# An edge product held in PSUM through its mish, in the first aggregation of a GNN kernel

## The chip, the cores and the metric

The kernel runs on one core of a Trainium2 chip. The metric is the device time of one execution in microseconds (us); the median of three runs of the kernel before is 4279.02 us.

## The reference, cut to what matters

The program is a graph network layer, a mixture of experts, a second graph layer and a second mixture, each added to the node features. The change touches the first stage of aggregation, in which two things are computed side by side: the weighted sum of neighbours of the first graph layer, and, for two thirds of the edges, the edge term `y` that only the second graph layer needs later.

```python
# first graph layer: aggregation of transformed nodes over the edges
msgs = support[edge_src] * edge_weight[:, None]
agg = segment_sum(msgs, edge_dst)
# second graph layer: the edge term
mish = lambda x: x * tanh(softplus(x))
y = mish(edge_features @ W_edge.T + b_edge)
```

With z the product plus its bias, the kernel writes tanh(softplus(z)) as 1 - 2/((1+e^z)^2 + 1). It stores (q - 1) * z, which is minus mish(z), where q = 2/((1+e^z)^2 + 1) is made by ScalarE from min(z, 20).

## The kernel before, in words

`stage_conv` is the stage. Its 106250 edges, sorted by target, are cut into groups of 512 (`CG` = 4 columns of 128). Six groups (`SLOTS`) make one round; there are 35 rounds (`IT`). For every group POOL gathers 4 times 128 rows of `support_table` into one of six buffers `gath` (line 509, 832 gathers), VectorE builds a matrix of edge weights at their targets (`one_hots`, lines 542 to 545), TensorE multiplies both into a PSUM tile `ps` (`segment`, line 655), and VectorE adds that tile to the running sums (`add`, line 537).

Between the groups stand four edge products per round (`MISH` = 4, numbered r = 0 to 3): TensorE multiplies a 512-edge block of edge features by `W_edge` into `ps_z[r % 2]` (`product`, line 664, 16 instructions in the profile). There are two such PSUM tiles; with three `ps` tiles and one for transposes they fill PSUM. VectorE then runs `mish_begin`: it adds the bias (line 523) from `ps_z` into the SBUF tile `neg[r]`, signals `z_free[r % 2]`, and clamps (line 525) from `neg[r]` into `q[r]`. ScalarE makes the factor in `q[r]` by four activations (lines 940 to 943). VectorE's `mish_end` multiplies (line 529) into `neg[r]`, which the queue of SP stores to memory (`store`).

The order is written out by hand, the same on each engine. In turn r of a round TensorE runs the groups `BEFORE[r]` (two groups when r is 0 or 2, one when r is 1 or 3) and then `product(r)`, which waits for `z_free[r % 2]`. VectorE, in its turn r, adds those groups, builds one-hots if r is odd, copies out 180 finished rows if r is 3 (`rows_of`, line 552), and then runs `mish_begin` of the product before, r-1, and `mish_end` of the one before that, r-2. At the start of a round VectorE also loads six addresses into registers (`places_of`, line 410). The first two rounds' products and round 0's groups are written out apart in `first()`, with n counting 0 to 7; there TensorE runs `product(n)` ahead of group n.

Of the kernel before, what the change touches and what calls it, by code (L numbers as in the profile page):

```python
# [10 lines left out]
ALU = mybir.AluOpType  # L11
# [3 lines left out]
P = 128  # L15
D = 256
# [10 lines left out]
CG = 4  # L27
# [9 lines left out]
MISH = len(KEPT)  # L37
# [14 lines left out]
ZMAX = 20.0  # L52
# [41 lines left out]
def take(eng, semaphore, n=1):  # L94

    eng.wait_ge(semaphore, n)
    eng.sem_inc(semaphore, -n)  # L97


def link(eng, ins, semaphore):  # L100

    ins.then_inc(semaphore, 1)
    take(eng, semaphore)
# [303 lines left out]
def places_of(nc, window, i, count, whole=False):  # L407

    at = window[0:1, bass.ds(i if whole else i * SLOTS, count)]
    return nc.values_load_multi_w_load_instructions(at, engines=[mybir.EngineType.DVE], min_val=0, max_val=NP)[1]  # L410


def stage_conv(nc, c, table):
# [4 lines left out]
    with ExitStack() as ctx:  # L418
# [9 lines left out]
        bias = sb("bias", [P, D])  # L428
        ln2 = sb("ln2", [P, 1])
        edge = [sb(f"edge{r}", [P, KD, CG * P]) for r in range(MISH)]  # L430
        q = [sb(f"q{r}", [P, CG, D]) for r in range(MISH)]
        neg = [sb(f"neg{r}", [P, CG, D]) for r in range(MISH)]
        ps = [pb(f"ps{n}", [P, W]) for n in range(3)]
        ps_z = [pb(f"pz{r}", [P, CG, D]) for r in range(2)]
# [12 lines left out]
        own, act_own, neg_own = sem("own"), sem("act_own"), sem("neg_own")  # L447
        w_in, act_free = sem("w_in"), sem("act_free")
        per_r = lambda n: [sem(f"{n}{r}") for r in range(MISH)]
        edge_in, edge_free, z_done, z_free = per_r("edge_in"), per_r("edge_free"), per_r("z_done"), [sem(f"z_free{n}") for n in range(2)]  # L450
        z_ready, q_ready, neg_ready, neg_out = per_r("z_ready"), per_r("q_ready"), per_r("neg_ready"), per_r("neg_out")
        block = ctx.enter_context(nc.Block(no_gpsimd_drain=True))

        def load_passes(eng):
            return eng.value_load(c.passes[0:1, 0:1], min_val=1, max_val=TW // W + 1)
# [59 lines left out]
        @block.vector  # L515
        def _(dve):
            def mish_begin(r):
                take(dve, z_done[r])
                dve.sem_inc(edge_free[r], 1)

                take(dve, neg_out[r], 16)

                link(dve, nc.vector.tensor_tensor(neg[r][:], ps_z[r % 2][:], bias[:].unsqueeze(1).to_broadcast([P, CG, D]), ALU.add), neg_own)
                dve.sem_inc(z_free[r % 2], 1)
                nc.vector.tensor_scalar(q[r][:], neg[r][:], ZMAX, None, ALU.min).then_inc(z_ready[r], 1)

            def mish_end(r):
                take(dve, q_ready[r])
                link(dve, nc.vector.scalar_tensor_tensor(neg[r][:], q[r][:], -1.0, neg[r][:], ALU.add, ALU.mult), neg_own)
                dve.sem_inc(neg_ready[r], 1)  # L530

            def add(places, s):
                take(dve, ps_ready[s % 3])
                dve.sem_inc(slot_free, 1)
                here = sums[:, bass.ds(places[s], W)]

                link(dve, nc.vector.tensor_tensor(here, here, ps[s % 3][:], ALU.add), own)
                dve.sem_inc(ps_free[s % 3], 1)

            def one_hots(i, half):  # L540
                part_of = lambda a: a[:, bass.ds(i * (SLOTS * CG) + half * HALF_COLS, HALF_COLS)]
                nc.vector.tensor_copy(at_hot[half][:, 0, :], part_of(rel))
                link(dve, nc.vector.tensor_copy(at_hot[half][:, 1, :], part_of(c.weight)), own)
                for j in range(HALF_COLS):
                    last = nc.vector.scalar_tensor_tensor(hot[half][:, j, :], c.iota[:], at_hot[half][:, 0, j:j + 1],
                                                          at_hot[half][:, 1, j:j + 1].to_broadcast([P, W]), ALU.is_equal, ALU.mult)
                last.then_inc(hot_ready[half], 1)

            def rows_of():
                take(dve, turned_ready)  # L550
                take(dve, rows_out, 16)
                link(dve, nc.vector.tensor_copy(rows[:], ps_t[:]), own)
                dve.sem_inc(rows_ready, 1)

            def step(i, behind):
                if behind:
                    dve.sem_inc(due, 1)
                places = places_of(nc, window, i, SLOTS)
                for r in range(MISH):
                    for s in BEFORE[r]:  # L560
                        add(places, s)
                    if behind and r == 3:
                        rows_of()
                    if r % 2:

                        one_hots(i + 1, r // 2)
                    mish_begin((r - 1) % MISH)
                    mish_end((r - 2) % MISH)

            def first():  # L570
                places = places_of(nc, window, 0, SLOTS)
                for n in range(2 * MISH):
                    if n < SLOTS:
                        add(places, n)
                    if n in (2, 5):

                        one_hots(1, n // 3)
                    if n >= 1:
                        mish_begin((n - 1) % MISH)
                    if n >= 2:  # L580
                        mish_end((n - 2) % MISH)

            for n in range(3):
                dve.sem_inc(ps_free[n], 1)
            for n in range(2):
                dve.sem_inc(z_free[n], 1)
            for r in range(MISH):
                dve.sem_inc(neg_out[r], 16)
            dve.sem_inc(rows_out, 16)
            nc.vector.memset(ln2[:], LN2)  # L590
            nc.vector.tensor_copy(rel[:], c.dstrel[:])
            link(dve, nc.vector.tensor_copy(window[:], c.base[:]), own)
            dve.sem_inc(act_free, 1)
            dve.wait_ge(w_in, 32)
            link(dve, nc.vector.memset(sums[:], 0.0), own)
            with dve.Fori(0, load_passes(dve)) as k:
                for half in range(2):
                    one_hots(0, half)
                first()
                for i in range(1, BEHIND):  # L600
                    step(i, False)
                with dve.Fori(BEHIND, IT - 1) as i:
                    step(i, True)
                places = places_of(nc, window, IT - 1, TAIL)
                add(places, 0)
                mish_begin(MISH - 1)
                add(places, 1)
                mish_end(MISH - 2)
                add(places, 2)
                add(places, 3)  # L610
                for m in range(IT - 1 - BEHIND, IT):
                    dve.sem_inc(due, 1)
                    if m == IT - BEHIND:
                        mish_end(MISH - 1)
                    rows_of()

                nc.vector.tensor_scalar(rel[:], rel[:], -float(W), None, ALU.add)
                link(dve, nc.vector.tensor_scalar(window[:], window[:], float(W), float(NP), ALU.add, ALU.min), own)
# [1656 lines left out]
```

## Time and profile before

| | |
|---|---|
| median of 3 runs | 4279.02 us (4276.55 to 4279.75) |
| profiled execution, span | 4272.1 us |
| its own time beside the span | not listed apart; the median is 6.9 us over the span |
| share of the span busy: PE, PEld, DVE, ACT, POOL | 82%, 72%, 54%, 45%, 66% |
| mean granted TensorE clock | 0.848 of 2.4 GHz |
| the stage of the change | first gather at 104.3 us, last at 1257.0 us; its last sums at 1264 us |

Engines: PE is TensorE's matmuls, PEld its weight loads, DVE is VectorE, ACT is ScalarE, POOL is GpSimd, SP the queue of transfers. The shares are averages over stages with different limits; for this change only the stretch from 104 to 1275 us matters, and what counts there is which wait ends last. The granted clock has two levels, 1.0 (2.4 GHz) and 0.5 (1.2 GHz); a mean between them says how much of a stretch was spent on each.

### The profile page before, as it was taken

The page shows a single profiled execution, that of the slowest core. Times are in us where ns is not written, and L with a number is a line of the kernel's source. Part 1 is how long each engine was busy: PE and PEld are TensorE (multiplying, and loading weights), DVE is VectorE, ACT ScalarE, POOL GpSimd, SP SyncE. Part 2 cuts the span into 40 slices and gives each one's busy share as a digit, 9 for nine tenths or more (in the row PEclk, how much of TensorE's full clock was granted, in tenths as well). Part 3 has the DMA queues.
Part 4 walks back from the last instruction along what each step waited for, and adds up shares of the span by engine and source line. Part 5 has one row for each costly group of instructions (what it writes and reads, how often), then busy time and mean ns, then how long its engine had stood idle before and what let it go on. Part 6 is the DMA issues. An engine that isn't in the chain of part 4 may idle for free. (4 is left out here: it accounts for less than half of the span.)

```text
span 4272.1 us, 68475 instructions
## 1 busy us (share of the span) xinstructions
PE 3514.0 (82%) x17723; PEld 3093.3 (72%) x17723; DVE 2295.0 (54%) x6976; ACT 1939.7 (45%) x3024; POOL 2823.4 (66%) x2732
## 2 busy tenths in 40 slices
PE   4777777777756899999999968888888888649999
PEld 4666666666645788888888867777777777538887
DVE  6566556556554445545445436666666666632222
ACT  4455555555541333333333445555555555423333
POOL 3677777777767777766676227777777777353444
PEclk7788788888776999999999987777777787559999
DMA  6455555555543222222222126666666666534443
GB/s 177 154 187 188 179 174 183 178 180 178 178 140 107 69 68 66 69 66 64 68 67 64 36 96 208 212 206 212 209 209 208 212 211 191 172 137 92 98 98 60
DMA packets 287817, 605.53 MB, mean 142 GB/s; under 512 B 61999, under 2 KB 163342, under 8 KB 287499
## 3 DMA queue, kind: packets, MB, share of 16 engines
q1 hardware_dynamic: 166267, 344.34, 25.0%
q0 software_dynamic: 114784, 245.67, 21.0%
q10 hardware_dynamic: 6576, 13.36, 0.9%
q8 instruction: 74, 1.21, 0.1%
q14 instruction: 116, 0.95, 0.1%
HBM read 460.33 MB, written 144.67 MB: 142 GB/s over the span
## 5 line engine op out<-in xcount | busy, mean ns | idle before, releaser
L1669 POOL DMA_INDIRECT y_node<-node_table,src_sb x832 | 847.6, 1019 | 379.2 <-issue 378.9
L509 POOL DMA_INDIRECT conv_gath<-support_table,src_sb x832 | 878.4, 1056 | 284.3 <-issue 259.9
L1110 POOL DMA_INDIRECT x_gath<-hidden_table,src_sb x832 | 792.9, 953 | 353.6 <-issue 259.9
L664 PE MATMUL conv_pz<-conv_we,conv_edge 128*128 128x256 f32 x2240 | 643.1, 451 | 76.9 <-PEq L97 76.7
L1682 PE MATMUL y_pa<-y_hot,y_node 128*128 128x64 f32 x3328 | 523.6, 326 | 181.7 <-PEq L97 181.1
L1682 PEld LDWEIGHTS y_pa<-y_hot,y_node 128*128 128x128 f32 x3328 | 506.8, 240 | 214.7 <-issue 212.0
L664 PEld LDWEIGHTS conv_pz<-conv_we,conv_edge 128*128 128x128 f32 x2240 | 510.2, 234 | 170.2 <-issue 81.4
L655 PE MATMUL conv_ps<-conv_hot,conv_gath 128*128 128x64 f32 x1664 | 255.6, 305 | 213.5 <-DMA conv_gath<-support_table,src_sb 210.9
L655 PEld LDWEIGHTS conv_ps<-conv_hot,conv_gath 128*128 128x128 f32 x1664 | 242.5, 219 | 245.9 <-DMA conv_gath<-support_table,src_sb 238.5
L1734 ACT ACTIVATE y_node<-y_node 128x1024 f32<-128x1024 f32 x208 | 219.4, 1056 | 340.6 <-ACTq L97 340.1
L1692 PE MATMUL y_pz<-y_we,y_edge 128*128 128x256 f32 x1104 | 361.0, 499 | 13.0 <-PEq L97 13.0
L940 ACT ACTIVATE conv_q<-conv_q 128x1024 f32<-128x1024 f32 x140 | 148.0, 1057 | 488.3 <-ACTq L97 488.3
L746 POOL DMA_INDIRECT out<-e_outs,e_node x112 | 175.0, 1562 | 281.5 <-POOLq L97 264.4
L1692 PEld LDWEIGHTS y_pz<-y_we,y_edge 128*128 128x128 f32 x1104 | 284.1, 264 | 69.2 <-issue 13.4
L1193 PE MATMUL x_ph<-x_xt,x_w 128*128 128x256 f32 (+1 forms) x1296 | 294.1, 371 | 0.5 <-PEq L97 0.3
L1199 PE MATMUL x_pm<-x_hid,x_w 128*128 128x256 f32 (+1 forms) x1296 | 289.7, 368 | 2.0 <-PEq L97 1.9
L1206 PE MATMUL x_py<-x_w,x_mid 128*128 128x256 f32 x1176 | 282.6, 381 | 1.6 <-PEq L97 1.6
L1321 ACT ACTIVATE x_hid<-x_ph,x_b 128x256 f32<-128x256 f32 (+1 forms) x324 | 129.0, 449 | 337.3 <-ACTq L97 337.0
L1127 PEld LDWEIGHTS x_ps<-x_hot,x_gath 128*128 128x128 f32 x1664 | 220.6, 201 | 74.4 <-DMA x_gath<-hidden_table,src_sb 46.3
L1804 DVE TENSOR_TENSOR y_node<-y_node,y_neg 128x256 f32<-128x256 f32 x556 | 199.7, 420 | 131.6 <-DMA y_node<-node_table,src_sb 131.6
L1127 PE MATMUL x_ps<-x_hot,x_gath 128*128 128x64 f32 x1664 | 217.9, 281 | 61.4 <-DMA x_gath<-hidden_table,src_sb 41.5
L1199 PEld LDWEIGHTS x_pm<-x_hid,x_w 128*128 128x128 f32 x1296 | 231.5, 196 | 28.7 <-issue 2.9
(256 smaller groups left out, 5844.8 us busy)
## 6 DMA issues: line engine op xcount, KB each, us to landing
conv_edge<-in_edge_t SPq DMA_DIRECT2D x140, 512.0 KB
edge_mish_table<-conv_neg SPq DMA_DIRECT2D x140, 512.0 KB
y_neg<-edge_mish_table SPq DMA_DIRECT2D x139, 512.0 KB, 4.2
y_edge<-in_edge_t SPq DMA_DIRECT2D x69, 512.0 KB
e_rows<-expert_rows SPq DMA_DIRECT2D x56, 272.0 KB, 3.3
conv_gath<-support_table,src_sb POOLq DMA_INDIRECT x832
x_gath<-hidden_table,src_sb POOLq DMA_INDIRECT x832
y_node<-node_table,src_sb POOLq DMA_INDIRECT x832, 3.1
```

Of the source, the lines that this page charges most:

```text
L509: pool.indirect_dma_start(gath[g % SLOTS][:, j, :], None, table[:, :], bass.IndirectOffsetOnAxis(ap=c.src[:, col:col + 1], axis=0),).then_ ...
L655: last = pe.matmul(ps[s % 3][:], gath[s][:, j, :], hot[half][:, at + j, :], start=j == 0, stop=j == CG - 1)
L664: last = pe.matmul(ps_z[r % 2][:, j, :], edge[r][:, m, j * P:(j + 1) * P], we[:, m, :], start=m == 0, stop=m == KD - 1)
L1110: pool.indirect_dma_start(gath[g % SLOTS][:, j, :], None, table[:, :], bass.IndirectOffsetOnAxis(ap=c.src[:, col:col + 1], axis=0),).then_ ...
L1127: last = pe.matmul(ps[n][:], gath[s][:, j, :], hot[half][:, at + j, :], start=j == 0, stop=j == CG - 1)
L1193: last = pe.matmul(ph[:, m, 0:width(u)], w_1[e][:, k, m * P:(m + 1) * P], xt[u % 2][:, k, 0:width(u)], start=k == 0, stop=k == KD - 1)
L1199: last = pe.matmul(pm[:, m, 0:width(u)], w_2[e][:, k, m * P:(m + 1) * P], hid[e % 2][:, k, 0:width(u)], start=k == 0, stop=k == KD - 1)
L1206: last = pe.matmul(py[:, s, :], mid[e % 2][:, k, s * P:(s + 1) * P], w_3[e][:, k, :], start=k == 0, stop=k == KD - 1)
L1669: pool.indirect_dma_start(node[g % SLOTS][:, j, :], None, c.t3[:, :], bass.IndirectOffsetOnAxis(ap=c.src[:, col:col + 1], axis=0),).then_i ...
L1682: last = pe.matmul(ps_a[s % RING][:, m, :], node[s][:, j, m * P:(m + 1) * P], hot[s % RING][:, j, :], start=j == 0, stop=j == CG - 1)
L1692: last = pe.matmul(ps_z[r][:, j, :], edge[r][:, m, j * P:(j + 1) * P], we[:, m, :], start=m == 0, stop=m == KD - 1)
L1734: act.activation(node[s][:], node[s][:], ACT.Relu, scale=-1.0).then_inc(msg_ready, 1)
```

## The change

The bias is added in place in PSUM, the clamp reads PSUM, and the last multiplication reads PSUM too; `neg[r]` is written only by that last multiplication. So `z_free` is signalled behind the last multiplication (`mish_end`) instead of behind the bias, and the wait for the previous store of `neg[r]` (`neg_out`) moves from `mish_begin` to `mish_end`. In `first()`, `mish_end(n-2)` moves ahead of the turn's `add`.

```diff
             def mish_begin(r):
                 take(dve, z_done[r])
                 dve.sem_inc(edge_free[r], 1)
-
-                take(dve, neg_out[r], 16)
-
-                link(dve, nc.vector.tensor_tensor(neg[r][:], ps_z[r % 2][:], bias[:].unsqueeze(1).to_broadcast([P, CG, D]), ALU.add), neg_own)
-                dve.sem_inc(z_free[r % 2], 1)
-                nc.vector.tensor_scalar(q[r][:], neg[r][:], ZMAX, None, ALU.min).then_inc(z_ready[r], 1)
+                z = ps_z[r % 2][:]
+                link(dve, nc.vector.tensor_tensor(z, z, bias[:].unsqueeze(1).to_broadcast([P, CG, D]), ALU.add), neg_own)
+                nc.vector.tensor_scalar(q[r][:], z, ZMAX, None, ALU.min).then_inc(z_ready[r], 1)

             def mish_end(r):
                 take(dve, q_ready[r])
-                link(dve, nc.vector.scalar_tensor_tensor(neg[r][:], q[r][:], -1.0, neg[r][:], ALU.add, ALU.mult), neg_own)
+                take(dve, neg_out[r], 16)
+                link(dve, nc.vector.scalar_tensor_tensor(neg[r][:], q[r][:], -1.0, ps_z[r % 2][:], ALU.add, ALU.mult), neg_own)
+                dve.sem_inc(z_free[r % 2], 1)
                 dve.sem_inc(neg_ready[r], 1)
...
             def first():
                 places = places_of(nc, window, 0, SLOTS)
                 for n in range(2 * MISH):
+                    if n >= 2:
+                        mish_end((n - 2) % MISH)
                     if n < SLOTS:
                         add(places, n)
...
                     if n >= 1:
                         mish_begin((n - 1) % MISH)
-                    if n >= 2:
-                        mish_end((n - 2) % MISH)
```

VectorE at the start of a round in the loop (turn r = 0: two adds, then bias and clamp of product 3, then the last multiplication of product 2), before:

```order
L537 TENSOR_TENSOR sums_table2<-sums_table2,conv_ps0 128x64
L537 ISA
L537 TENSOR_TENSOR sums_table2<-sums_table2,conv_ps1 128x64
L523 TENSOR_TENSOR conv_neg3<-conv_pz1,conv_bias 128x1024
L525 TENSOR_SCALAR conv_q3<-conv_neg3 128x1024
L529 SCALAR_TENSOR_TENSOR conv_neg2<-conv_q2,conv_neg2 128x1024
```

and now:

```order
L536 TENSOR_TENSOR sums_table2<-sums_table2,conv_ps0 128x64
L536 ISA
L536 TENSOR_TENSOR sums_table2<-sums_table2,conv_ps1 128x64
L521 TENSOR_TENSOR conv_pz1<-conv_pz1,conv_bias 128x1024
L522 TENSOR_SCALAR conv_q3<-conv_pz1 128x1024
L527 SCALAR_TENSOR_TENSOR conv_neg2<-conv_q2,conv_pz0 128x1024
```

The instructions keep their order, but the tile `pz0` of product 2, which `product(0)` is to write next, is now read by the last row, behind two adds and the whole `mish_begin` of product 3.

VectorE in `first()`, the turn of n = 4 (the ISA row sets an address), before:

```order
L537 ISA
L537 TENSOR_TENSOR sums_table<-sums_table,conv_ps 128x64
L523 TENSOR_TENSOR conv_neg<-conv_pz,conv_bias 128x1024
L525 TENSOR_SCALAR conv_q<-conv_neg 128x1024
L529 SCALAR_TENSOR_TENSOR conv_neg<-conv_q,conv_neg 128x1024
```

and now:

```order
L527 SCALAR_TENSOR_TENSOR conv_neg<-conv_q,conv_pz 128x1024
L536 ISA
L536 TENSOR_TENSOR sums_table<-sums_table,conv_ps 128x64
L521 TENSOR_TENSOR conv_pz<-conv_pz,conv_bias 128x1024
L522 TENSOR_SCALAR conv_q<-conv_pz 128x1024
```

The last multiplication now opens the turn, ahead of the add, and the bias and clamp of the following product come behind it.

## Rows read from the trace of the kernel before

**Rows 1.** The page: its first line, and the gathers' group (count | busy us, mean ns | idle us).

```profile
span 4272.1 us, 68475 instructions
...
L509 POOL DMA_INDIRECT conv_gath<-support_table,src_sb x832 | 878.4, 1056 | 284.3 <-issue 259.9
```

**Rows 2.** One line's instructions, the gathers: duration in ns, minimum/median/maximum.

```profile
L509 POOL DMA_INDIRECT conv_gath<-support_table,src_sb x832: 938/944/1535, 104.3 to 1257.0; - x167
```

**Rows 3.** Windows: stretch, length, PE, PEld, DVE, ACT, POOL busy, clock, DMA, GB/s.

```profile
300.00:400.00 100.00, 75.93 (x353) 65.43 (x354) 60.49 (x144) 56.00 (x54) 77.73 (x74) 0.85 0.55 180
3700.00:3780.00 80.00, 55.78 (x248) 51.88 (x248) 63.64 (x423) 35.07 (x80) 60.80 (x64) 0.50 0.45 159
```

**Rows 4.** Groups of VectorE by line and shape, whole span.

```profile
L523 DVE TENSOR_TENSOR conv_neg<-conv_pz,conv_bias 128x1024 f32<-128x1024 f32 x140 | 170.6, 1218 | 40.0 <-DVEq L97 40.0
L529 DVE SCALAR_TENSOR_TENSOR conv_neg<-conv_q,conv_neg 128x1024 f32<-128x1024 f32 x140 | 170.5, 1218 | 2.5 <-DVEq L97 2.5
...
L525 DVE TENSOR_SCALAR conv_q<-conv_neg 128x1024 f32<-128x1024 f32 x140 | 98.8, 706 | 33.9 <-DVEq L97 33.9
...
L1819 DVE TENSOR_TENSOR y_po<-y_po,y_bo 90x512 f32<-90x512 f32 x33 | 22.7, 687 | 4.3 <-DVEq L97 4.3
L1820 DVE TENSOR_SCALAR y_qo<-y_po 90x512 f32<-90x512 f32 x33 | 22.7, 687 | 4.9
...
L1480 DVE TENSOR_SCALAR x_q<-x_z 128x512 f32<-128x512 f32 x22 | 9.7, 440 | 5.3 <-DVEq L97 5.3
```

**Rows 5.** Timeline of PE in `first()`: start us, duration us, group, [idle before].

```profile
128.60 3.69 PE L664 MATMUL conv_pz<-conv_we,conv_edge 128*128 128x256 f32 x16 [2.63 <-PEq L97]
...
148.60 6.69 PE L664 MATMUL conv_pz<-conv_we,conv_edge 128*128 128x256 f32 x16 [2.62 <-PEq L97]
155.13 1.00 PE L655 MATMUL conv_ps<-conv_hot,conv_gath 128*128 128x64 f32 x8
158.75 6.74 PE L664 MATMUL conv_pz<-conv_we,conv_edge 128*128 128x256 f32 x16 [2.62 <-PEq L97]
...
181.96 3.67 PE L664 MATMUL conv_pz<-conv_we,conv_edge 128*128 128x256 f32 x16
...
190.53 6.21 PE L664 MATMUL conv_pz<-conv_we,conv_edge 128*128 128x256 f32 x16 [4.05 <-PEq L97]
```

**Rows 6.** Timeline of DVE in the same turn of `first()`.

```profile
156.45 0.22 DVE L537 TENSOR_TENSOR sums_table<-sums_table,conv_ps 128x64 f32 x1 [6.08 <-DVEq L97]
157.23 1.22 DVE L523 TENSOR_TENSOR conv_neg<-conv_pz,conv_bias 128x1024 f32<-128x1024 f32 x1 [0.56 <-DVEq L97]
158.70 0.69 DVE L525 TENSOR_SCALAR conv_q<-conv_neg 128x1024 f32<-128x1024 f32 x1 [0.24 <-DVEq L97]
159.31 1.22 DVE L529 SCALAR_TENSOR_TENSOR conv_neg<-conv_q,conv_neg 128x1024 f32<-128x1024 f32 x1
```

**Rows 7.** Timeline of ACT there: the first and the last of four activations.

```profile
159.51 1.06 ACT L940 ACTIVATE conv_q<-conv_q 128x1024 f32<-128x1024 f32 x1 [5.48 <-ACTq L97]
...
163.04 1.15 ACT L943 ACTIVATE conv_q<-conv_q,conv_ln 128x1024 f32<-128x1024 f32 x1
```

**Rows 8.** Timeline of DVE in the loop: turn 3, the round's start, turn 1.

```profile
813.84 0.22 DVE L537 TENSOR_TENSOR sums_table<-sums_table,conv_ps 128x64 f32 x1 [1.79 <-DVEq L97]
...
818.11 1.21 DVE L523 TENSOR_TENSOR conv_neg<-conv_pz,conv_bias 128x1024 f32<-128x1024 f32 x1
...
827.55 0.22 DVE L537 TENSOR_TENSOR sums_table<-sums_table,conv_ps 128x64 f32 x1 [6.12 <-DVEq L97]
...
832.91 0.22 DVE L537 TENSOR_TENSOR sums_table<-sums_table,conv_ps 128x64 f32 x1 [0.52 <-DVEq L97]
...
836.31 1.21 DVE L523 TENSOR_TENSOR conv_neg<-conv_pz,conv_bias 128x1024 f32<-128x1024 f32 x1
```

**Rows 9.** Timeline of PE and DVE at the stage's end: last product, last add.

```profile
1239.97 3.67 PE L664 MATMUL conv_pz<-conv_we,conv_edge 128*128 128x256 f32 x16
...
1263.97 0.22 DVE L537 TENSOR_TENSOR sums_table<-sums_table,conv_ps 128x64 f32 x1 [6.79 <-DVEq L97]
```

**Rows 10.** Timeline of POOL in `first()`: a gather beside line 523, one beside line 529.

```profile
157.80 0.94 POOL L509 DMA_INDIRECT conv_gath<-support_table,src_sb  x1 [0.30 <-issue]
159.05 1.16 POOL L509 DMA_INDIRECT conv_gath<-support_table,src_sb  x1 [0.30 <-issue]
```

## The prediction

> **What bounds the kernel now.** Look first at the page for the span, 4272.1 us, and at the gathers' group [rows 1]: 832 gathers of 1056 ns on POOL. Their own line [rows 2] says when the stage begins and ends, 104.3 to 1257.0 us, and that a gather takes 944 ns at the median but up to 1535. A window in the middle [rows 3] holds 74 gathers per 100 us, each followed by about 0.3 us of issue [rows 10], so POOL is without a break at its work, while PE is busy 76 us, DVE 60 and ACT 56. The stage is bound by gathers. A round of 24 gathers takes 24 / 0.74 = 32.4 us; from product 8 at 181.96 us to the last at 1239.97 [rows 5, 9] there are 131 turns in 1058.0 us, 32.3 us per round of four.
>
> Then ask why PE and DVE don't bind it. PE may run one product ahead: `ps_z` has two tiles, and a tile is free as soon as the bias has been read from it. So `product(r)` runs while DVE is still at the adds, one-hots and mish of turn r. That overlap is what the change touches. How it looks without overlap can be seen in `first()`, where PE waits in each turn for DVE's bias [rows 5, 6]: product at 148.60, its group ends at 156.13, add at 156.45, bias at 157.23, and only 0.30 us after the bias ends, the next product, at 158.75.
>
> **The change, step by step.**
>
> *Where the tile comes free.* In turn r, `product(r)` needs the tile of product r-2. Before, that was freed in turn r-1, by the bias. Now it is freed by the last multiplication, which on DVE stands at the very end of turn r: behind the adds of turn r's groups, the one-hots, and `mish_begin(r-1)`. But the groups of turn r+1 come behind `product(r)` on PE. So PE waits for the whole of DVE's turn, then DVE waits for PE's product and groups: the two engines take turns, in every turn of the loop. This is a chain that can be summed from rows.
>
> PE's part: a product of length p, then 0.84 us to the end of one group (155.29 to 156.13), 1.68 for two, then 0.32 us until the add starts [rows 5, 6]. DVE's part from the add to the bias: 0.78 us in turns 0 and 2 [rows 6]; 3.40 us in turn 1, which builds one-hots (832.91 to 836.31); 4.27 us in turn 3, which also copies rows (813.84 to 818.11) [rows 8]. From the bias to the next product: 1.46 us to the clamp's start, the clamp c less 0.08 us that the next instruction overlaps it, 1.22 us for the last multiplication, 0.30 us to the product [rows 5, 6].
>
> *The clamp c.* From SBUF it takes 706 ns for 1024 elements. From PSUM the same operation takes 687 ns for 512, where 512 from SBUF take 440 [rows 4]. 1024 elements should then cost what line 523 costs, whose two lengths are 687 and 1218. I take 1.22 us; the bounds are 0.70 and 1.22. The bias in place costs nothing more: line 1819 does it in PSUM at 687 ns for 512, the same length as its clamp. The last multiplication stays at 1.22: an operand in PSUM (line 523) and operands in SBUF alone (line 529) both take 1218 [rows 4]. The Trainium skill says otherwise (VectorE: DVE Perf Modes, on the TRN2 errata): reading PSUM has a fixed part of 120 cycles against 58. By that rule this multiplication would grow by 65 ns, some 9 us over the stage; the two equal rows speak against it, and I leave it out.
>
> So from bias to product it is 1.46 + 1.14 + 1.22 + 0.30 = 4.12 us, and the turns are p + 6.90 (turns 0 and 2), p + 8.68 (turn 1), p + 9.55 (turn 3): a round is **4p + 32.0 us**. The six register loads of a round's start (6.12 us idle before 827.55 [rows 8]) now lie beside product 3 and its following groups, p + 1.7 us, and cost nothing while that is longer.
>
> *The length p of a product.* 16 matmuls take 3.67 us at the full clock [rows 9] and, at half of it, twice that, 7.34. Now PE pauses between its bursts for 5.2 us (0.32 + 0.78 + 4.12) to 8.7 us in every turn. In `first()`, products that follow a pause of 2.6 to 4.1 us took 6.69, 6.74 and 6.21 us, and once 3.69; the group behind such a product then takes 1.00 us, so the clock has risen by its end [rows 5]. All the new pauses are longer, so I expect every product to begin at the half clock: p = 6.4, within 5.5 to 7.0. A round takes 57.6 us instead of 32.3.
>
> *First rounds.* Product 2 now waits for ScalarE's factor of product 0: instead of 0.30 us after the bias ended it starts after 0.24 + 1.22 + 0.12 + 4.68 + 0.30 + 1.22 + 0.30 = 8.08 us (ScalarE's four activations are 159.51 to 164.19 [rows 7]); 128.60 [rows 5] becomes 136.4. Each of the next four turns is p + 11.2 us by the same links, two of them 2.6 longer for one-hots; the turn to product 7 has no group to wait for and takes 9.1 us; the turn to product 8 is p + 6.9. Product 8 starts at 202.6 + 5p = 234.6 us instead of 181.96, **+52.6**.
>
> *The loop.* 131 turns, 32 rounds and three turns: 32 × 57.6 + 44.3 = 1888 us instead of 1058.0, **+830**.
>
> *The end.* Before, the last groups waited for their gathers, and the last add came 24.0 us after the last product's start [rows 9]. Now POOL is far ahead; by the links above the last add comes after about 14.5 us, **-9.5**.
>
> *What costs nothing.* The wait for the store (`neg_out`) moves behind the factor; that store was issued a whole round, 57 us, before. SP's loads and stores keep their order and have a longer round. ScalarE's 4.7 us lie beside the next product and its groups, over 7 us, and the adds behind them. POOL waits for buffers more, which hurts nobody. The later stages are not touched.
>
> Sum: +873 us on the profiled span of 4272.1 gives 5145; the median stands 6.9 us above that span, so **5150 us**.
>
> **The rivals.**
>
> *Faster, through POOL.* The last multiplication has two SBUF operands, and a gather beside it takes 1.16 us where one beside the bias takes 0.94 [rows 10]. The change leaves one SBUF operand, and takes the clamp's source out of SBUF. If all gathers fell to the median, 832 × (1056 - 944) ns = 93 us would go, and the time would be 4186. It decides only while gathers bind the stage: the round must stay under 24 × 1.24 = 29.9 us. The chain has 32.0 us before any product is counted. The Trainium skill has the rule (SBUF — State Buffer, on the two sides of SBUF): VectorE and GpSimd share a pair of ports, held by one of them for a whole instruction, when VectorE works from SBUF in its fast mode or with two SBUF inputs. The longer gather agrees with that. I give this 3%; the gathers may well shorten, unseen.
>
> *No change.* If the waits were covered as before, by the tile order being other than I read it, gathers would still bind: 4279. The order of both engines shows the freeing row last in its turn. 1%.
>
> *Slower, at the full clock.* If the pauses don't lower the clock, p = 3.67 and 2.73 us × 136 products = 371 us less: 4780. For it speaks the one product of 3.69 us after a pause; against it the three others, and longer pauses. 5%.
>
> *Slower, at the half clock throughout.* In 3700 to 3780 us the clock is 0.50 all along, though PE is busy 56 of 80 us [rows 3]. If here too it never rises, p = 7.34 and each of six groups takes 0.84 us more: 128 + 33 × 5.0, some 295 us more: 5445. Against it: after each long product in `first()` the group ran at the full clock. 6%.
>
> **How the numbers follow.** My forecast has 85%: turns taken, p near 6.4. One us of p is 136 us, so p of 5.5 to 7.0 gives -122 to +82; the clamp at 0.70 would give -70. The range is 5020 to 5245; it leaves out the four rivals, 15%, and a few per cent of the forecast's own. A measurement of this kernel can tell about 0.2%, 9 us, from no change. Slower by more than that: the forecast and the two clocks, 0.96; faster 0.03; same 0.01.
>
> **What would show it.** In the profile after: the stage ends near 2140 us; 42 gathers per 100 us instead of 74, with POOL waiting for the add (`slot_free`) instead of issuing on; rounds of 57 to 58 us; a pause of 5 to 9 us on PE before every product, and products of 6 to 7 us; the clamp at 1.22 us, bias and last multiplication unchanged; a granted clock of about 0.7 in the stage, and the gathers' mean nearer to 944 ns. The prediction is wrong if products overlap DVE's turns, or if the round is under 46.7 us (4 × 3.67 + 32.0).

## The result, and the profile after

The changed kernel takes **5054.5 us** (four runs, 5049.6 to 5061.3) where the kernel before takes 4279.4 (with a fourth run): a ratio of 1.181, 95% interval 1.180 to 1.183. Forecast were 5150 us and a range of 5020 to 5245. It is slower, by the mechanism that was forecast, and 95 us less slow than the sum said.

The page of the changed kernel, its first line, against [rows 1], and the gathers' line with what ended the idle time before them, against [rows 2]:

```profile
span 5047.9 us, 68475 instructions
```

```profile
L509 POOL DMA_INDIRECT conv_gath<-support_table,src_sb x832: 942/947/1066, 105.6 to 2003.9; - x167
its engine sat idle before it (us, times) until:
  DVEq L533: 897.9, 134
```

The last add of the stage comes at 2034.5 us instead of 1264.0, 770 us later, and that is nearly all: the spans differ by 775.8 us. Line 533 is the release of a gather buffer by VectorE's add. POOL, which issued almost without a break before (284.3 us idle, 259.9 of them its own issue), now waits 898 us for that release. Gathers no longer bind.

A window of the loop, to set beside [rows 3] (columns as there):

```profile
600.00:700.00 100.00, 54.62 (x216) 45.73 (x217) 37.26 (x76) 35.19 (x34) 41.71 (x44) 0.74 0.35 113
```

Every engine is less busy than before, PE 55 us of 100 instead of 76, POOL 42 instead of 78. When all engines idle more and the stage is longer, look for a chain that goes through them in turn. The timeline of PE in the loop shows its half (start, duration, group, [idle before]):

```profile
1001.45 1.00 PE L654 MATMUL conv_ps<-conv_hot,conv_gath 128*128 128x64 f32 x8
1010.37 5.48 PE L663 MATMUL conv_pz<-conv_we,conv_edge 128*128 128x256 f32 x16 [7.92 <-PEq L97]
1015.68 1.89 PE L654 MATMUL conv_ps<-conv_hot,conv_gath 128*128 128x64 f32 x16
1017.42 0.38 PE L669 MATMUL conv_pt<-ident_sb,conv_hid 128*90 128x128 f32 x2
1022.60 6.18 PE L663 MATMUL conv_pz<-conv_we,conv_edge 128*128 128x256 f32 x16 [4.80 <-PEq L97]
1028.62 1.00 PE L654 MATMUL conv_ps<-conv_hot,conv_gath 128*128 128x64 f32 x8
1038.20 5.22 PE L663 MATMUL conv_pz<-conv_we,conv_edge 128*128 128x256 f32 x16 [8.59 <-PEq L97]
1043.26 1.90 PE L654 MATMUL conv_ps<-conv_hot,conv_gath 128*128 128x64 f32 x16
1050.18 6.04 PE L663 MATMUL conv_pz<-conv_we,conv_edge 128*128 128x256 f32 x16 [5.03 <-PEq L97]
```

and the timeline of DVE in the same turn has the other half:

```profile
1017.01 0.22 DVE L536 TENSOR_TENSOR sums_table<-sums_table,conv_ps 128x64 f32 x1 [6.93 <-DVEq L97]
1017.90 0.22 DVE L536 TENSOR_TENSOR sums_table<-sums_table,conv_ps 128x64 f32 x1 [0.67 <-DVEq L97]
1018.57 1.23 DVE L521 TENSOR_TENSOR conv_pz<-conv_pz,conv_bias 128x1024 f32<-128x1024 f32 x1 [0.44 <-DVEq L97]
1019.95 1.23 DVE L522 TENSOR_SCALAR conv_q<-conv_pz 128x1024 f32<-128x1024 f32 x1
1021.09 1.21 DVE L527 SCALAR_TENSOR_TENSOR conv_neg<-conv_q,conv_pz 128x1024 f32<-128x1024 f32 x1
```

Read both together. PE runs a product (1010.37) and the next turn's groups, to 1017.57; DVE, idle for 6.93 us, starts its adds at 1017.01, when the first group is done; bias, clamp and last multiplication follow with hardly a gap to 1022.30; 0.30 us later PE starts the next product, after 4.80 us of nothing. The three steps from 1010.37 on are 12.23, 15.60 and 11.98 us, and the one before 1010.37 is 14.8; a round takes 54.6 us (32 rounds from product 8 at 231.2 us), where it took 32.35.

The groups of VectorE, against [rows 4] (count | busy us, mean ns):

```profile
L521 DVE TENSOR_TENSOR conv_pz<-conv_pz,conv_bias 128x1024 f32<-128x1024 f32 x140 | 171.7, 1226 | 32.1 <-DVEq L97 32.1
L522 DVE TENSOR_SCALAR conv_q<-conv_pz 128x1024 f32<-128x1024 f32 x140 | 171.4, 1225 | 20.9 <-DVEq L97 0.2
L527 DVE SCALAR_TENSOR_TENSOR conv_neg<-conv_q,conv_pz 128x1024 f32<-128x1024 f32 x140 | 169.5, 1211 | 31.3 <-DVEq L97 31.3
```

Of the three only the clamp is longer, 1225 ns instead of 706. And the gathers became shorter:

```profile
L509 POOL DMA_INDIRECT conv_gath<-support_table,src_sb x832 | 788.8, 948 | 1119.5 <-DVEq L533 897.9 <-issue 221.6
```

948 ns at the mean, where it was 1056.

### The profile page after: what moved, and what is told of

Its sections match the earlier page's. It is cut to its first block and busy times, and to the rows that moved or that the text cites. A ratio compares the mean times of both kernels' runs of the same rounds, so it can differ in the third digit from the quotient of the medians.

```text
span 5047.9 us, 68475 instructions
## 1 busy us (share of the span) xinstructions
PE 3623.9 (72%) x17723; PEld 3168.1 (63%) x17723; DVE 2373.6 (47%) x6976; ACT 1939.8 (38%) x3024; POOL 2739.3 (54%) x2732
## 5 line engine op out<-in xcount | busy, mean ns | idle before, releaser
L663 PE MATMUL conv_pz<-conv_we,conv_edge 128*128 128x256 f32 x2240 | 803.7, 536 | 940.2 <-PEq L97 940.2
L509 POOL DMA_INDIRECT conv_gath<-support_table,src_sb x832 | 788.8, 948 | 1119.5 <-DVEq L533 897.9
L663 PEld LDWEIGHTS conv_pz<-conv_we,conv_edge 128*128 128x128 f32 x2240 | 618.2, 283 | 1092.7 <-issue 959.1
L536 DVE TENSOR_TENSOR sums_table<-sums_table,conv_ps 128x64 f32 x208 | 46.2, 222 | 1035.3 <-DVEq L97 1035.3
L1205 PEld LDWEIGHTS x_py<-x_w,x_mid 128*128 128x128 f32 x1176 | 223.2, 192 | 32.0 <-issue 2.1
```

The source lines that it names most:

```text
L509: pool.indirect_dma_start(gath[g % SLOTS][:, j, :], None, table[:, :], bass.IndirectOffsetOnAxis(ap=c.src[:, col:col + 1], axis=0),).then_ ...
L663: last = pe.matmul(ps_z[r % 2][:, j, :], edge[r][:, m, j * P:(j + 1) * P], we[:, m, :], start=m == 0, stop=m == KD - 1)
L1205: last = pe.matmul(py[:, s, :], mid[e % 2][:, k, s * P:(s + 1) * P], w_3[e][:, k, :], start=k == 0, stop=k == KD - 1)
```

## The experiments

Nine kernels ran besides. The first four ask what the price is made of: the late freeing, the operands in PSUM, or the clock.

**The late freeing alone.** Bias to SBUF, clamp and last multiplication from SBUF as before; only `z_free` moves behind the last multiplication (and `first()` keeps the changed kernel's order). Against the changed kernel:

```diff
-                z = ps_z[r % 2][:]
-                link(dve, nc.vector.tensor_tensor(z, z, bias[:].unsqueeze(1).to_broadcast([P, CG, D]), ALU.add), neg_own)
-                nc.vector.tensor_scalar(q[r][:], z, ZMAX, None, ALU.min).then_inc(z_ready[r], 1)
+                take(dve, neg_out[r], 16)
+                link(dve, nc.vector.tensor_tensor(neg[r][:], ps_z[r % 2][:], bias[:].unsqueeze(1).to_broadcast([P, CG, D]), ALU.add), neg_own)
+                nc.vector.tensor_scalar(q[r][:], neg[r][:], ZMAX, None, ALU.min).then_inc(z_ready[r], 1)
...
-                take(dve, neg_out[r], 16)
-                link(dve, nc.vector.scalar_tensor_tensor(neg[r][:], q[r][:], -1.0, ps_z[r % 2][:], ALU.add, ALU.mult), neg_own)
+                link(dve, nc.vector.scalar_tensor_tensor(neg[r][:], q[r][:], -1.0, neg[r][:], ALU.add, ALU.mult), neg_own)
                 dve.sem_inc(z_free[r % 2], 1)
```

> The kernel before with only the freeing of the product's PSUM tile moved behind the last multiplication; bias still goes to SBUF, clamp and last multiplication still read SBUF. Theory (the tile is freed at the end of VectorE's turn, so TensorE and VectorE take turns): the round keeps the chain of the change less 0.52 us per turn for the shorter clamp, 54.6 - 2.1 = 52.5 us, time 4985 (4940 to 5055), gathers again at a mean near 1056 ns. Rival (the operands in PSUM cost the time): near the kernel before, 4280 to 4300.

Measured: 5046.0 us, ratio 1.178 (1.176 to 1.181). With no operand of the change in PSUM, practically the whole loss is there. The rival that the operands cost the time falls. The gathers' mean was 1018 ns, not near 1056, which costs nothing here, where POOL waits. But the 0.52 us per turn that the shorter clamp gives back did not come: the round is 54.5 us, as long as with the long clamp. The timeline of PE says where it went:

```profile
1007.15 5.98 PE L662 MATMUL conv_pz<-conv_we,conv_edge 128*128 128x256 f32 x16 [7.38 <-PEq L97]
...
1019.45 6.64 PE L662 MATMUL conv_pz<-conv_we,conv_edge 128*128 128x256 f32 x16 [4.38 <-PEq L97]
...
1034.98 5.71 PE L662 MATMUL conv_pz<-conv_we,conv_edge 128*128 128x256 f32 x16 [8.05 <-PEq L97]
```

Each pause is about half a microsecond shorter than in the changed kernel, and each product about half a microsecond longer (mean in the loop 6.19 us instead of 5.74). The granted clock over the product at 1007.15 is 0.61, over the changed kernel's product at 1010.37 it is 0.67: what VectorE saved, TensorE spent at the half clock. Why the two cancel so closely, these runs don't show.

**Freeing earlier in the same turn.** One exchange in the changed kernel's loop:

```diff
-                    mish_begin((r - 1) % MISH)
                     mish_end((r - 2) % MISH)
+                    mish_begin((r - 1) % MISH)
```

> The changed kernel with one exchange in the loop: in each turn the last multiplication of product r-2, which frees the tile, comes ahead of the bias and clamp of product r-1 instead of behind them; no operation is added or taken away. Theory: TensorE gets its tile some 2.5 us sooner in each turn and VectorE's bias and clamp fall beside the product, round near 45 us, time 4740 (4680 to 4830). Rival (operands in PSUM, or the moved wait for the store): unchanged, 5040 to 5065.

Measured: 4661.0 us, ratio 1.089 (1.086 to 1.091), a round of 42.6 us. The same operations, with the freeing two instructions sooner, win back 393 us, half of the loss. So the place of the freeing in the turn sets the time. The gain is larger than the range, 4680 to 4830. The round is 12.0 us shorter. Its part without the four products fell from 31.7 to 21.5 us, 2.5 us per turn as expected; the other 1.8 us are shorter products, whose mean in the loop fell from 5.74 us to 5.29:

```profile
1008.77 5.37 PE L663 MATMUL conv_pz<-conv_we,conv_edge 128*128 128x256 f32 x16 [5.21 <-PEq L97]
...
1018.41 5.38 PE L663 MATMUL conv_pz<-conv_we,conv_edge 128*128 128x256 f32 x16 [2.32 <-PEq L97]
...
1030.69 6.35 PE L663 MATMUL conv_pz<-conv_we,conv_edge 128*128 128x256 f32 x16 [6.07 <-PEq L97]
```

**Keeping TensorE busy in the pause.** Matmuls into spare columns of a group tile, ahead of each product. In the first try each of them was two of the profile's instructions, not one as I had counted:

```diff
+                    for f in range((18, 32)[r % 2]):
+                        pe.matmul(ps[(2, 0)[r % 2]][:, 256:512], we[:, f % 2, 0:P], we[:, f % 2, :], start=True, stop=True)
                     product(r)
```

> The changed kernel with matmuls of no use in TensorE's pause ahead of each product in the loop (18 in turns 0 and 2, 32 in turns 1 and 3, into spare columns of an accumulation bank). Theory with the clock as a part of the price: TensorE stays at the full clock, a product falls from a mean of 5.74 us to 3.67, round 4 x 3.67 + 31.7 = 46.4 us, time 4785 (4740 to 4860). Rival (the clock has no part): 5050 or longer. Rival (the clock is the whole price): 4280 to 4330.

Measured: 5310.2 us, ratio 1.240 (1.238 to 1.243). Every product of the loop took 3.62 us, so the clock stayed up, but the filling took 7.9 and 14 us and overran the pauses; the total says nothing. The second try has `(9, 15)` in place of `(18, 32)`:

> As the filled pause, with half the matmuls (9 in turns 0 and 2, 15 in turns 1 and 3; each is two of the profile's instructions, so they take 3.9 and 6.5 us and fit into the pauses of 5.0 and 7.9 us, where the first filling took 7.9 and 13.9 and overran them). Theory with the clock as a part of the price: every product near 3.65 us, round 4 x 3.65 + 31.7 = 46.3 us instead of 54.6, time 4780 (4750 to 4830). Rival (the clock has no part): 5050.

Measured: 4824.3 us, ratio 1.128 (1.125 to 1.131). Its PE timeline (line 679 is the filling):

```profile
1003.16 3.69 PE L663 MATMUL conv_pz<-conv_we,conv_edge 128*128 128x256 f32 x16 [1.39 <-PEq L97]
...
1008.64 4.05 PE L679 MATMUL conv_ps<-conv_we 128*128 128x256 f32 x18
1013.61 3.69 PE L663 MATMUL conv_pz<-conv_we,conv_edge 128*128 128x256 f32 x16 [0.92 <-PEq L97]
...
1017.97 6.69 PE L679 MATMUL conv_ps<-conv_we 128*128 128x256 f32 x30
1026.72 5.38 PE L663 MATMUL conv_pz<-conv_we,conv_edge 128*128 128x256 f32 x16 [2.06 <-PEq L97]
```

Matmuls of no use make the kernel 230 us faster. Three of four products are at 3.69 us; with the loop's mean of 3.99 the chain of the prediction gives 4 × 3.99 + 31.7 = 47.7, and the round is 47.64. So at least 230 of the 775 us are the half clock, and most of the rest is the taking of turns at the full clock. (The one longer product, 5.38 us, follows the turn in which 2.06 us were left idle.)

**A third tile.** The changed kernel with three product tiles; the groups keep one tile instead of three, and the loop is unrolled by three rounds.

```diff
-        ps = [pb(f"ps{n}", [P, W]) for n in range(3)]
-        ps_z = [pb(f"pz{r}", [P, CG, D]) for r in range(2)]
+        ps = [pb("ps", [P, 512])]
+        ps_z = [pb(f"pz{r}", [P, CG, D]) for r in range(3)]
```

> The changed kernel with three PSUM tiles for products instead of two (the groups' tiles go from three to one to make room; loop unrolled by three). All operands stay in PSUM as changed, the tile is still freed by the last multiplication. Theory: product r needs the tile of r-3, freed a turn earlier, so TensorE and VectorE overlap again; the round is the longer of 24 gathers (24 x 1.25 = 30 us) and VectorE's own turn, which with the longer clamp and the register loads sums to about 33.6 us; time 4325 (4270 to 4400). Rival (operands in PSUM or the moved wait are the price): 4900 or more.

Measured: 4531.0 us, ratio 1.058 (1.056 to 1.060): 523 us come back, 200 fewer than I expected, and the time is outside the range. To see what the rest is, a control has the same layout and loop, with operands and freeing of the kernel before:

> The layout of the three tiles (three product tiles, one group tile, loop unrolled by three), with operands and freeing of the kernel before: bias to SBUF, clamp and last multiplication from SBUF, tile freed by the bias. Theory: what three tiles left over against the kernel before (4531 against 4281) comes from the single group tile and the unrolled loop, so the control is near 4531 less some 50 to 70 us for the shorter clamp: 4470 (4430 to 4530). Rival (operands in PSUM and the late freeing still cost some 250 us there): 4281 to 4320.

Measured: 4466.6 us, ratio 1.045 (1.043 to 1.047). So with a third tile the change costs some 60 us. That is near the longer clamp (0.52 us × 4 × 33 = 69), but the traces divide it otherwise. Product 8 starts 19 us later than in the control (191.2 us, not 172.1): in the first rounds TensorE still waits for the last multiplication, 5.0 to 7.7 us ahead of products 3 to 6, where the control pauses 2.8 us at most. The 131 turns of the loop take 47 us more (1297.1, not 1250.4), and only there can the longer clamp be the cause.

The remaining 190 us belong to the layout. With one group tile PE waits at a round's start for an add that stands behind VectorE's register loads; in this control:

```profile
1012.35 0.22 DVE L537 TENSOR_TENSOR sums_table<-sums_table,conv_ps 128x64 f32 x1 [5.21 <-DVEq L97]
1012.87 1.94 PE L655 MATMUL conv_ps<-conv_hot,conv_gath 128*128 128x64 f32 x8 [9.42 <-PEq L97]
```

And once in three rounds, where the unrolled loop jumps back, VectorE's idle time before the round's first add is 7.1 to 8.4 us, where it is about 3.6 or 5.2 in the other two. The two parts of the layout were not tried apart.

**Can the shorter gathers be had without holding the product's tile?** Two kernels each take one part, from the kernel before. The first moves the clamp to ScalarE:

```diff
-                nc.vector.tensor_scalar(q[r][:], neg[r][:], ZMAX, None, ALU.min).then_inc(z_ready[r], 1)
+                dve.sem_inc(z_ready[r], 1)
...
+                link(act, act.activation(now, neg[r][:], ACT.Relu, scale=-1.0, bias=top[:]), act_own)
+                link(act, act.activation(now, now, ACT.Exp, scale=-1.0, bias=top[:]), act_own)
```

> The kernel before with the clamp moved from VectorE to ScalarE (one activation more for each product, as 20 - relu(20 - z)); bias and last multiplication as before. VectorE loses 0.61 us per turn, 2.4 us of its 31.9 per round. Theory (gathers bind, 24 x 1.356 = 32.5 us per round): little, 4265 (4245 to 4285). Rival (VectorE's turn binds as much): 33 x 2.4 = 80 us less, 4200.

Measured: 4234.9 us, ratio 0.990 (0.989 to 0.992). The second lets ScalarE's last activation write a PSUM tile, which the last multiplication reads:

```diff
-                act.activation(now, now, ACT.Exp, scale=-1.0, bias=ln2[:]).then_inc(q_ready[r], 1)
+                take(act, pq_free)
+                act.activation(pq[:], now, ACT.Exp, scale=-1.0, bias=ln2[:]).then_inc(q_ready[r], 1)
```

> The kernel before with ScalarE's last activation written to a PSUM tile of its own, so that the last multiplication has one SBUF operand (two group tiles instead of three, the transposes share a bank with one). Gathers near 955 ns instead of 1056, 24 x 1.25 = 30 us per round. Theory (VectorE's own turn of 31.9 us is close behind the gathers): little, 4265 (4240 to 4285). Rival (gathers alone bind): 33 x 2.3 = 76 us less, 4205.

Measured: 4228.2 us, ratio 0.989 (0.987 to 0.991). Both theories missed: the kernels gained 41 and 48 us against the kernel before, where the theories gave little and the rivals 80 and 76. Their gathers, the first kernel's and the second's:

```profile
L509 POOL DMA_INDIRECT conv_gath<-support_table,src_sb x832 | 833.8, 1002 | 284.4 <-issue 257.5
```

```profile
L511 POOL DMA_INDIRECT conv_gath<-support_table,src_sb x832 | 817.7, 983 | 277.6 <-issue 252.2
```

A mean of 1002 ns with the clamp off VectorE and of 983 with the multiplication changed, so both operations stretch gathers. In both POOL still issues almost without a break, and 832 × 54 ns = 45 us and 832 × 73 ns = 61 us are not far from what the kernels gained. So gathers bind, as the first theory had it; what it left out is that the clamp stretches them. The second kernel's mean stayed at 983 ns, where near 955 was expected. VectorE's turn is no fixed 31.9 us: in the second kernel, where VectorE has the same operations, a round takes 30.9 us (31.1 in the first, 32.35 in the kernel before).

Both parts together:

> Both: clamp on ScalarE and factor in PSUM. Theory (gathers and VectorE's turn bind one behind the other): only now the round falls, to some 30.5 us, time 4220 (4200 to 4250), below both kernels. Rival (something else binds): 4265 or more.

Measured: **4215.0 us**, ratio 0.985 (0.984 to 0.987), in the range, and below both kernels, though by only 13 us to the second: the second's fastest run took 4218.2 us, this one's slowest 4218.5. That only now the round falls was wrong: it is 30.6 us, and most of the way was made by either part alone. Its gathers and a window:

```profile
L511 POOL DMA_INDIRECT conv_gath<-support_table,src_sb x832 | 789.4, 949 | 303.9 <-issue 243.5 <-DVEq L537 60.4
```

```profile
300.00:400.00 100.00, 79.05 (x355) 67.25 (x356) 53.99 (x135) 72.32 (x69) 74.75 (x80) 0.80 0.58 188
```

80 gathers per 100 us instead of 74, each 949 ns: the relief that the change gave POOL, without holding a product's tile. Of the 832 × 107 ns = 89 us that the gathers save, 61 reach the total; POOL now waits 60.4 us for VectorE's add (line 537), where it waited 24 in the kernel before.

## Why the prediction was right, step by step

*The mechanism.* Right: the tile freed at the end of VectorE's turn makes the two engines take turns. The freeing alone gives the loss, moving it within the turn halves the loss, and a third tile leaves some 60 us of the change's own price. The links of the chain hold one by one: without p, the turns from 1010.37 on and the one before take 6.75, 9.42, 6.76 and 8.76 us, where 6.90, 9.55, 6.90 and 8.68 were forecast.

*The first rounds.* Product 8 started at 231.2 us instead of 181.96: +49.2, forecast +52.6. *The end* of the stage and what follows gave -5.4, forecast -9.5.

*The loop.* 131 turns took 1790 us instead of 1058: +732, forecast +830. Here lies the miss, in one term: **p, the length of a product, which I took as 6.4 us and which is 5.74**. That is 0.66 × 131 = 86 us. The chain of the rest, 4p + 32.0, came out as 54.61 - 4 × 5.74 = 31.7, another 12 us. That every product begins at the half clock was right: the clock is 0.50 from 1010.37 to 1014.00 us and 1.00 from 1014.20 to the product's end, the other products of the loop begin and end the same way, and 0.74 is granted in the window above (forecast about 0.7). I had taken p from products after pauses of 2.6 to 4.1 us and supposed that longer pauses make no difference once the clock is down. In this loop they go with shorter products: after pauses of 7.9 and 8.6 us products take 5.2 to 5.5 us, after 4.8 to 5.0 us they take 6.0 to 6.2. But that is no rule: in the first rounds of the same kernel products after pauses of 10.2 to 13.1 us take 5.1 to 6.5 us, and with the freeing alone the loop's mean is 6.19. What sets the point within a product at which the clock rises, no run here shows. That p fell inside its bounds of 5.5 to 7.0 is what kept the total in the range.

*The clamp.* 1225 ns, forecast 1.22 us from the half-sized row. The bias in place, 1226 ns, and the last multiplication, 1211, are as forecast. By the rule of the Trainium skill that was weighed (VectorE: DVE Perf Modes, on the TRN2 errata) the multiplication should, by the prediction's estimate, have grown by 65 ns with an operand in PSUM. It did not: it measured 1218 ns before.

*The rivals.* The faster one was right in its mechanism and, as said, decided nothing: gathers fell to 948 ns, nearly the 944 of the bound, but POOL then waited 898 us. The clocks: neither full nor half throughout, as said. The waits that I costed at nothing do cost nothing: VectorE idles before the last multiplication in 8 of 140 cases, 31.3 us in all, six of them in the first rounds and two behind the last product, so the wait for the store never shows in the loop. And at the median the next product starts 0.30 us behind that multiplication, 0.52 at most, so SP's loads don't hold it.

## What to carry to other kernels

An engine's buffer should be freed by the earliest instruction that can free it; a change that lets a later one do so must be judged by what stands in front of that later instruction on its engine, not by the length of the instruction. Count tiles against the turn: with two tiles, freeing at the very end of the next turn left no overlap here, and freeing two instructions sooner brought half of the loss back. And when a chain makes TensorE pause, price its work at the clock that it will have then, and sweep that price, since it can eat a saving elsewhere whole.

## What was not expected of the hardware

A saving on VectorE of 0.52 us in every turn gave nothing, because the products grew by 0.45 us each: pause plus product stayed nearly the same, and the round stayed at 54.5 us. That is what the rows show; why it comes out so evenly is open. In the same way 4 to 6.7 us of useless matmuls per turn made the kernel 4.6% faster. And a gather on POOL is stretched by two kinds of VectorE's instructions, the clamp from SBUF to SBUF and the multiplication of two SBUF operands: taking away either leaves 1002 or 983 ns of 1056, taking away both 949. In the trace of the kernel before, gathers beside neither of the two take about 950 ns at the mean, those beside the multiplication alone 1337. That is the rule on the shared pair of ports that the prediction named (the Trainium skill, SBUF — State Buffer, on the two sides of SBUF), and here the gathers' numbers agree with it. Of the other direction, VectorE held by a gather, little shows: the clamp of the kernel before takes 694 ns at the median and 939 at most, though gathers run almost throughout.
